# A GRU kernel whose candidate scan writes its sums to PSUM in place of SBUF

## What is computed

```python
def step(hprev, gxt):
    gh = hprev @ whh.T + bhh
    r = jax.nn.sigmoid(gxt[:, :h] + gh[:, :h])
    z = jax.nn.sigmoid(gxt[:, h:2 * h] + gh[:, h:2 * h])
    n = jnp.tanh(gxt[:, 2 * h:] + r * gh[:, 2 * h:])
    hn = (1.0 - z) * n + z * hprev
    return (hn, hn)
...
fwd = _bigru(x_inner, f_wih_fw, ...)
bwd = jnp.flip(_bigru(jnp.flip(x_inner, 1), b_wih_fw, ...), 1)
y = jax.nn.silu(fwd + bwd) * jax.nn.silu(z)
y = jnp.einsum('bld,cd->blc', y, w_out).reshape(B, H, W, C)
return x + y
```

## Time and profile before

| | before |
|---|---|
| time, median of 3 runs | 1243.77 us |
| lowest and highest run | 1241.73, 1247.79 us |
| the profiled execution, as reported | 1242.83 us |
| its span from the first to the last instruction | 1241.1 us |
| mean granted TensorE clock over the span | 0.585 |
| recurrence of L2 | 434.2 us |
| recurrence of L3 | 435.1 us |

### The profile page before, as it was taken

One profiled execution on the slowest core, in us unless ns is written; L12 is line 12 of the kernel. 1 busy time (PEld: TensorE's weight loads), 2 busy tenths in 40 slices (PEclk: granted clock), 3 DMA queues, 4 the chain that ended last, 5 costly groups with the idle time before them and its releaser, 6 DMA issues. The chain is left out here.

```text
span 1241.1 us, 56119 instructions
## 1 busy us (share of the span) xinstructions
PE 1066.6 (86%) x22390; PEld 814.7 (66%) x22390; DVE 931.8 (75%) x5703; ACT 665.8 (54%) x4269; POOL 116.7 (9%) x96
## 2 busy tenths in 40 slices
PE   3778799768999999999999968899999999999985
PEld 2555254355777777777777755677777777777775
DVE  3553799984777777777777785677777777777776
ACT  4224620007666666666666654666666666666663
POOL 1001389910000000000000001000000000000000
PEclk9587899957555555555555557655555555555555
DMA  4000500000000000000000000000000000000000
GB/s 117 2 8 5 129 1 1 1 5 2 4 4 3 4 4 4 3 4 4 4 4 3 4 2 5 3 4 4 4 4 3 4 4 4 3 4 4 4 3 27
DMA packets 8225, 12.63 MB, mean 10 GB/s; under 512 B 5745, under 2 KB 7121, under 8 KB 7674
## 3 DMA queue, kind: packets, MB, share of 16 engines
q1 hardware_dynamic: 7962, 9.05, 2.9%
HBM read 8.26 MB, written 0.79 MB: 7 GB/s over the span
## 5 line engine op out<-in xcount | busy, mean ns | idle before, releaser
L1123 PE MATMUL L3s_early<-L3s_h_hi,L_w_hidden 97*128 97x8 f16 x4096 | 195.3, 177 | 38.7 <-DVE L3s_h_hi L1037 5.2
L1123 PE MATMUL L2s_early<-L2s_h_hi,L_w_hidden 97*128 97x8 f16 x4096 | 195.3, 177 | 37.8 <-DVE L2s_h_hi L1037 5.4
L1123 PEld LDWEIGHTS L3s_early<-L3s_h_hi,L_w_hidden 97*128 97x128 f16 x4096 | 148.8, 105 | 111.2 <-DVE L3s_h_hi L1037 81.8
L1123 PEld LDWEIGHTS L2s_early<-L2s_h_hi,L_w_hidden 97*128 97x128 f16 x4096 | 148.8, 105 | 110.0 <-DVE L2s_h_hi L1037 77.4
L1037 DVE TENSOR_TENSOR_SCAN L3s_h_hi<-L3s_renew,L3s_terms 96x32 f16<-96x32 f32 x512 | 113.2, 221 | 84.8 <-ACT L3s_terms L1077 59.1
L1037 DVE TENSOR_TENSOR_SCAN L2s_h_hi<-L2s_renew,L2s_terms 96x32 f16<-96x32 f32 x512 | 113.2, 221 | 83.8 <-ACT L2s_terms L1077 57.4
L1077 ACT ACTIVATE L3s_terms<-L3s_cand 96x16 f32<-96x16 f32 x512 | 111.5, 218 | 106.0 <-DVE L3s_cand L1022 105.9
L1077 ACT ACTIVATE L2s_terms<-L2s_cand 96x16 f32<-96x16 f32 x512 | 111.5, 218 | 104.7 <-DVE L2s_cand L1022 104.6
L1123 PE MATMUL L3s_early<-L3s_h_lo,L_w_hidden 96*128 96x8 f16 x2048 | 131.0, 174 | 0.2 <-DVE L3s_h_lo L1045 0.2
L1123 PE MATMUL L2s_early<-L2s_h_lo,L_w_hidden 96*128 96x8 f16 x2048 | 130.9, 174 | 0.2 <-DVE L2s_h_lo L1045 0.2
L1123 PE MATMUL L2s_late<-L2s_h_hi,L_w_hidden 97*128 97x8 f16 x2048 | 130.0, 174 | 0.0
(11 more groups left out here) (243 smaller groups left out, 2477.7 us busy)
## 6 DMA issues: line engine op xcount, KB each, us to landing
L_wih_raw<-in_L_wih SPq DMA_DIRECT2D x2, 1152.0 KB, 11.0
l_w_raw<-in_L_w SPq DMA_DIRECT2D x1, 1296.0 KB
L_w_hidden_raw<-in_L_whh SPq DMA_DIRECT2D x2, 576.0 KB
stream<-in_x SPq DMA_DIRECT2D x2, 384.0 KB, 3.8
out<-stream SPq DMA_DIRECT2D x4, 192.0 KB, 2.1
l_idft<-in_idft SPq DMA_DIRECT2D x1, 400.0 KB
rpe_lw<-in_rpe_lw SPq DMA_DIRECT2D x1, 384.0 KB
l_dft<-in_dft SPq DMA_DIRECT2D x1, 288.0 KB, 2.9
```

Of the source, the lines that this page charges most:

```text
L1123: return e.matmul(dst, weights.hidden[0:rows, wp, GATES * (2 * g + j) + gate, :], rhs, start=False, stop=False, skip_group_check=True)
```

## The change

The SBUF tile `cand` goes. In its place `cand(g, p, x)` names 32 columns in block 3 of the group's current `early` bank, as 96 x 32 fp32: columns 0 to 31 of the block for even steps, 32 to 63 for odd ones. The candidate scan writes there, and the tanh reads every second element from there. No wait, no semaphore, no order and no number of instructions changes.

```diff
@@ gru_steps
         reset = pairs("reset", [C, 2, PER, 2])
-        cand = pairs("cand", [C, 2, PER, 2])
         keep = pairs("keep", [C, 2, PER])
@@
         keep_sum = lambda g, p: late[g][p][:, 0]
+        cand = lambda g, p, x: early[g][p][0:C, 3].rearrange("p c s -> p (c s)")[:, x * 2 * PER:(x + 1) * 2 * PER]
@@ candidate
-                    e.tensor_tensor_scan(flat(cand[g][:, x]), flat(reset[g][:, x]), flat(cand_sum(g, p)[0:C, :, :, s]), 0.0,
+                    e.tensor_tensor_scan(cand(g, p, x), flat(reset[g][:, x]), flat(cand_sum(g, p)[0:C, :, :, s]), 0.0,
                                          ALU.mult, ALU.add).then_inc(cand_ready[g], 1)
@@ scalar
                         e.wait_ge(cand_ready[g], q + 1)
-                        e.activation(terms[g][:, x, :, 0], cand[g][:, x, :, 1], ACT.Tanh).then_inc(activated[g], 1)
+                        e.activation(terms[g][:, x, :, 0], cand(g, p, x).rearrange("p (c k) -> p c k", k=2)[:, :, 1], ACT.Tanh).then_inc(activated[g], 1)
```

## The result

| | before | after |
|---|---|---|
| median of 4 runs | 1245.78 us | 1230.48 us |
| lowest and highest run | 1241.73, 1248.25 | 1229.65, 1231.9 |
| span of the profiled execution | 1241.1 | 1227.9 |

The ratio is 0.9882, with a 95% interval of 0.9849 to 0.9914: 1.2% faster, 1245.8 - 1230.5 = 15.3 us by the medians and 14.7 by the ratio, where 31.7 were forecast. (The 1243.77 that stands ahead of the prediction is the median of the first three of these four runs of before.) 1230.5 lies inside the range of 1197 to 1251, but the gain is less than half of the forecast.

What follows compares the result with a forecast made beforehand. VectorE's cycle through both groups was taken to bound the recurrences; 36 ns off the tanh less 5 for the scan, twice a step over 512 steps, gave 31.7 us off 1243.8: 1212 us, range 1197 to 1251.

Steps and rivals of the forecast that it cites:

- What bounds the kernel: Both recurrences: VectorE's written order, the two groups taking turns, with ScalarE's tanh in it twice; 1.68 us a step.
- (a): Tanh on ScalarE: reading PSUM in place of SBUF takes it from 218 to about 182 ns, 36 less.
- (b): Candidate scan on VectorE: writing PSUM in place of SBUF costs an extra 5 ns, between scan's start and tanh's.
- D: Extra cost of the candidate scan's write to PSUM; taken as 5 ns, outer ends -36 and +36.
- (c): Instructions queued behind the candidate scan: kept_part of group 0 keeps 0.05 of 0.08 us cover before h_hi.
- (d): What is late next: 31 ns off each half-step; TensorE's group loop keeps slack, taking over only from 70 ns.
- Sum: Both recurrences: 2 x 31 ns x 512 steps = 31.7 us off, giving 1212 us, 2.6% faster.
- group loop binds: Rival: a group's own loop is already as tight as VectorE's, so one gain a step: 15.9 us, 1228; chance 0.07.
- The rule against the change: Skill's overheads for VectorE, about 60 ns on SBUF and 125 on PSUM: kernel slower, about 1267 us.

Runs made afterwards that it cites:

- kept_first_psum: The changed kernel with group 0's kept_part put ahead of group 1's remainder on VectorE: 1226.76 us, ratio 0.9849.
- one_wait_psum: The changed kernel with kept_part counting on the tanh's semaphore, so h_hi has one merged wait in place of two: 1210.2 us, ratio 0.9716.
- cand1_first_one_wait: The changed kernel with the merged wait, and group 1's candidate scan put ahead of group 0's remainder: 1274.15 us, ratio 1.0228.

## Why the prediction fell short

**What bounds the kernel** held: VectorE's cycle through both groups, with TensorE beside it. After the change the scans of the candidate still find their reset ready.

**(a) and (b)** held: 36 ns off the tanh, and D of 8 where 5 was taken. That alone moves the forecast from 31.7 to 2 x 28 x 512 = 28.7.

**(c) is the step that failed.** It priced the hand-over from kept_part to h_hi at 0.03 us, by the tanh's, and so found 0.08 us of cover in group 0. The hand-over is 0.10, since kept_part's wait is a separate instruction; the cover was zero. The 0.27 us between the starts stood in the earlier trace rows and could have been asked about: 0.16 + 0.03 do not make 0.27, and there was a second candidate for what ended last. I had put the whole 0.27 down to the tanh because the tanh's own 0.25 fitted. Two inputs of h_hi came due together, and only one of them got earlier.

**(d)** held in its arithmetic: the group loop did not take over. Its slack was right too, as the 214 ns and the 1653 against 1654 of kept_first_psum show. The 0.04 and 0.06 us that it left for groups 1 and 0 are what one_wait_psum has, where both halves do get shorter: the reset sigmoid starts 254 and 274 ns ahead of the scan there, 40 and 60 more than 214.

**Sum.** 2 x 31 should have read 28 + 0. The result, 14.7 us, lies by chance near the 15.9 of the rival *group loop binds*, but by another mechanism: both come to one half-step of the two. The reset sigmoid of group 1 is 286 ns ahead of its scan after the change, 72 more than the 214 of a loop that binds, so the group loop does not bind.

**The rule against the change**, from the Trainium skill (Perfetto Trace Analysis, Optimizing Scalar/DVE Operations), gave VectorE 65 ns more on PSUM. No run here shows it: writing cost about 8 ns, and for reading the rows have 677 ns against 680 for the add, and 200 with one input in PSUM against 204 with both in SBUF for the scan. The same section's figures for ScalarE, 42 ns less on PSUM, agree with the 36.

The merged wait gives the version that beats both kernels: 1210.2 us.

## What to carry to other kernels

Before a gain on one input of an instruction is counted, work out for every other input when it comes due, with the hand-over measured for that input; where the parts of such a distance don't add up to it, something unseen stands between. In these kernels an instruction that waits for two semaphores has the one written second as a wait instruction of its own. That costs next to nothing where the other wait ends later (215 ns against 213 in group 1), and 68 ns where the separate one ends last. So write first the wait that will end last, which then rides on the instruction, or let both producers count on one semaphore. And ahead of an instruction that must run early, place nothing in the same queue that waits for another group.

## What was not expected of the hardware

- A write to PSUM cost VectorE's scan of 32 elements only 8 to 9 ns more than one to SBUF, and reading the same bank at the same time nothing.
- A separate wait in VectorE's queue takes 21 ns in its row and adds 68 ns between the end of the producer and the start: 101 in place of 33.
- Two steps of every 32 were longer, by some 240 and 46 ns in L2 and 350 and 70 in L3, while VectorE's stream held two such waits a step, and none was with them gone; they cost 5.7 us before the change and 5.8 after it. The cause is not shown.
- Two queued VectorE instructions start 67 to 142 ns apart, far less than the 150 to 225 that each is shown to last, and the distance depends on what stands ahead: remainder to kept_part is 93 in the changed kernel and 67 in cand1_first_one_wait, where the scan in front of them came after a wait; the scan to the remainder is 114 in the one and 137 in the other.
